# First token tile's queries alone in the opening, values turned in their own bank, GpSimd makes the context's low parts

## The reference

```python
q = (layernorm(x) @ Wq)            # 512 tokens, 32 heads of 16
k, v = context @ Wk, context @ Wv  # per batch 512 keys, 8 heads of 16
x = x + softmax(q k^T / 4) v @ Wo
x = x + self_attention(layernorm(x))      # 2nd layer: rope, causal, 32 heads on 8
w = block_dequantize_3bit(q3, norm)       # (bits / 7) * (2 n) - n
x = x + layernorm(x) @ w.T + bias
```

## Time and profile before

| | us |
|---|---|
| median of 3 runs | 336.38 (335.36 to 337.74) |
| profiled execution | 338.57 |
| span of its instructions | 336.7 |
| PE busy in it | 312.5 (93%) |
| DVE, ACT, POOL busy | 228.4, 186.6, 111.0 |

### The profile page before, as it was taken

How to read it: one execution, slowest core, us unless ns; L and a number is a source line. 1 busy time by engine, 2 the same in 40 slices (tenths; PEclk the granted TensorE clock), 3 DMA queues, 4 the chain that set the end, 5 groups by cost and what they waited for, 6 DMA issues and landing times.

```text
span 336.7 us, 7756 instructions
## 1 busy us (share of the span) xinstructions
PE 312.5 (93%) x2662; PEld 217.2 (64%) x2665; DVE 228.4 (68%) x391; ACT 186.6 (55%) x368; POOL 111.0 (33%) x200
## 2 busy tenths in 40 slices
PE   6699939969999999999999999999999998999996
...
GB/s 212 412 191 22 135 112 74 202 181 86 180 118 188 180 104 197 185 88 200 184 92 205 182 117 227 181 156 201 146 0 5 2 6 6 9 6 8 2 31 93
DMA packets 39466, 41.48 MB, mean 123 GB/s; under 512 B 19936, under 2 KB 34272, under 8 KB 37216
## 3 DMA queue, kind: packets, MB, share of 16 engines
...
## 4 chain that ended last, share of the span: by engine, by line
PE 70%; DVE 12%; DMA 7%; ACT 4%; issue 3%; POOL 2%; SPq 1%; DVEq 0%; ACTq 0%; POOLq 0%
PE b_d L1001 8%; PE b_c L1059 7%; DMA kstack<-kparts 5%; PE b_v L976 4%; PE b_s L1022 4%; PE b_c L1187 4%; PE b_v L977 4%; PE b_v L978 4%; PE b_k L976 3%; PE b_k L978 3%; PE b_k L977 3%; PE b_x L1022 3%; DVE negmax L783 3%; DMA wkv_raw<-in_L_xattn_Wv_dram 2%; DVE vaug L773 2%
## 5 line engine op out<-in xcount | busy, mean ns | idle before, releaser
L591 ACT ACTIVATE region<-b_c 128x512 f32<-128x512 f32 x128 | 74.6, 597 | 46.3 <-PE b_c L1059 26.2
L783 DVE TENSOR_REDUCE negmax<-b_s 128x1 f32<-128x512 f32 x72 | 49.7, 690 | 49.4 <-PE b_s L1022 48.4
L1059 PE MATMUL b_c<-qstack,kstack 108*128 108x128 bf16 x512 | 50.6, 222 | 0.0
L795 DVE TENSOR_TENSOR cT_l<-cx,cT_h 128x512 fp32r<-128x512 f32 x56 | 45.1, 805 | 6.9 <-ACT cT_h L611 6.8
L1059 PEld LDWEIGHTS b_c<-qstack,kstack 108*128 108x128 bf16 x512 | 32.5, 98 | 26.6 <-issue 13.9
L976 PE MATMUL b_k<-cT_h,wkv_h 128*128 128x512 f32 x64 | 36.3, 568 | 7.8 <-DVE cT_l L827 4.2
L477 POOL TENSOR_TENSOR mwide<-negmax,zeros 128x4 bf16<-128x4 f32 x32 | 6.4, 199 | 101.4 <-DVE negmax L783 101.4
L783 DVE TENSOR_REDUCE negmax<-b_x 128x1 f32<-128x512 f32 x56 | 38.2, 681 | 0.9 <-PE b_x L1022 0.8
L976 PE MATMUL b_v<-cT_h,wkv_h 128*128 128x512 f32 x64 | 35.7, 558 | 1.6 <-DVE vaug L773 1.2
L611 ACT ACTIVATE cT_h<-cx 128x512 fp32r<-128x512 f32 x56 | 35.0, 628 | 0.0
L1022 PE MATMUL b_s<-kstack,qstack 96*128 96x512 bf16 x72 | 28.1, 391 | 6.4 <-DMA kstack<-kparts 3.3
(11 more groups left out here) (357 smaller groups left out, 584.7 us busy)
## 6 DMA issues: line engine op xcount, KB each, us to landing
...
```

The costliest lines, as they stand in the source:

```text
L591: nc.scalar.activation(pT[:, g], b_c[g % 2][:].rearrange("p (a n) -> p a n", a=KT), ACT.Exp, scale=SCALE).then_inc(exp_ready, 1)
L783: nc.vector.tensor_reduce(negmax[:, n % 2, g:g + 1], score_bank(n, g, trip)[:], AX, ALU.max, negate=True).then_inc(max_ready, 1)
L795: nc.vector.tensor_tensor(cT_l[:, c], cx[:, m % 2, c], cT_h[:, c].bitcast(F32), ALU.subtract).then_inc(ctx_low, 1)
L1059: last = nc.tensor.matmul(b_c[g % 2][:, P * a:P * a + P], kstack[0:ROWS, m % 4, g, P * a:P * a + P], qstack[0:ROWS, g, m % 4], start=True, ...
```

## The change

Four things are changed together.

- **Opening.** x is loaded in two DMAs, the first token tile alone. Only its queries are made ahead of slot 0 (`first_queries_of(0, ...)`, 16 matmuls of 128 columns); those of tiles 1 to 3 follow in slot 0, half a tile in each of its steps 0 to 5. A token tile holds four batches, so the first stacks are now six DMAs of 128 KB for batches 0 to 3 at once. Three chunks of batch 1's projections, the unpacking of the weights and the split of batch 1's keys move into slot 0. ACT converts batch 0's chunks 2 and 3 without waiting for the value weights.
- **Values.** `vT` is turned into bank `b_t` at g=5 (`turn_values`), DVE copies that bank at g=6. The next values in `b_v` wait for `vT` and no longer for DVE's copy. In the last slots `b_v` is used as before.
- **Context rests.** The operation on `cT_l` of batches 2 to 15 moves from DVE to POOL (`low_context`): chunk 0 at the start of POOL's slot, chunk 1 behind the keys' parts, chunks 2 and 3 behind the first half's maxima.
- **Weights.** DVE unpacks to 2q/7 - 1, and POOL multiplies once, in four parts, behind slot 1's work.

The diff, cut to what the text speaks of:

```diff
 
-            return g == 1 and (looped(trip) or 1 <= n < B - 1)
+            return g == 1 and (looped(trip) or n < B - 1)
 
         def wait_queries(eng, m, trip):
 
...
+                    eng.dma_start(qstack[HD * s:HD * s + HD].rearrange("p g b n -> p g (b n)"),
+                                  qparts[:, part, 0:BPT].rearrange("p b r t -> p (b r t)")).then_inc(first_queries, 16)
...
+        def value_bank(n, trip):
+
+            return b_t if looped(trip) or n < B - 2 else b_v
...
-                sp.dma_start(xs[:], xf).then_inc(x_loaded, 16)
+                sp.dma_start(xs[:, 0], xf[:, 0]).then_inc(x_loaded, 16)
                 sp.dma_start(xwq, xwq_d.rearrange("(c p) r n -> p c r n", p=P)).then_inc(xwq_loaded, 16)
+                sp.dma_start(xs[:, 1:TILES], xf[:, 1:TILES]).then_inc(xs_loaded, 16)
                 load_ctx(1, 0)
-                sp.wait_ge(ctx_low, C)
-                load_ctx(2, 0)
                 sp.dma_start(q3[:], q3_d.rearrange("(t p g) k -> p t (g k)", t=TILES, p=P)).then_inc(packed_loaded, 16)
-                sp.dma_start(wnorm[:, 0].rearrange("p (t g) -> p t g", t=TILES),
+                sp.dma_start(wnorm[:].rearrange("p (t g) -> p t g", t=TILES),
                              norm_d.rearrange("(t p g) a -> p t (g a)", t=TILES, p=P)).then_inc(packed_loaded, 16)
                 for i in range(2):
                     sp.dma_start(kstack[STACK:ROWS, i].bitcast(I32), sel_d).then_inc(first_sel, 16)
                 for part, done in enumerate((k_high, k_mid, k_low)):
                     sp.wait_ge(done, 1)
                     stack_keys(0, part)
-
+                sp.wait_ge(ctx_low, C)
+                load_ctx(2, 0)
+                for part, done in ((0, q_high), (2, q_low)):
+                    sp.wait_ge(done, 1)
+                    first_queries_part(sp, part)
                 sp.wait_ge(ctx_low, 2 * C)
                 load_ctx(3, 0)
-                for part, done in ((0, q_high), (2, q_low)):
-                    sp.wait_ge(done, R)
-                    first_queries_part(sp, part, 0, 1, first_queries)
-                for part in range(3):
-                    first_queries_part(sp, part, 1, 4, next_queries)
 
             def slot(n, trip):
                 if not looped(trip):
@@ -412,6 +417,8 @@
                     for part, done in enumerate((k_high, k_mid, k_low)):
                         sp.wait_ge(done, split)
                         stack_keys(m, part)
+                if not looped(trip) and n == 1:
+                    sp.wait_ge(q_low, TILES)
...
+            def low_context(m, c, trip):
+
+                if live(m, trip):
+                    wait(pool, ctx_high, C, m, c + 1, trip)
+                    if not looped(trip) and (m, c) == (2, 0):
+                        pool.wait_ge(ctx_low, 2 * C)
+                    nc.gpsimd.tensor_tensor(cT_l[:, c], cx[:, m % 2, c], cT_h[:, c].bitcast(F32), ALU.subtract).then_inc(ctx_low, 1)
+
             def slot(n, trip):
+                low_context(n + 2, 0, trip)
                 if live(n - 1, trip):
                     max_parts(n - 1, 1, trip)
                 if splits_keys(n, 1, trip):
                     key_parts(n + 1, trip)
+                low_context(n + 2, 1, trip)
                 if n == B - 1:
                     low_keys_values()
                 if live(n, trip):
                     max_parts(n, 0, trip)
+                low_context(n + 2, 2, trip)
+                low_context(n + 2, 3, trip)
+                if not looped(trip) and n == 1:
+                    pool.wait_ge(unpacked, 1)
+                    for t in range(TILES):
+                        scale_weights(t)
                 if n == B - 2:
...
-                pool.wait_ge(w_scaled, 1)
-                pool.wait_ge(unpacked, 1)
-                nc.gpsimd.tensor_tensor(wide, wide, wnorm[:, 1].unsqueeze(2).to_broadcast([P, NGRP, GS]), ALU.mult).then_inc(w_step, 1)
-                key_parts(1, 0)
-                pool.wait_ge(w_step, 1)
-                nc.gpsimd.tensor_tensor(wide, wide, wnorm[:, 0].unsqueeze(2).to_broadcast([P, NGRP, GS]), ALU.subtract).then_inc(w_ready, 1)
 
             opening()
             slots(pool, slot, 2)
...
+                    if not looped(trip) and n == 0 and g in (2, 4, 6):
+                        query_high(g // 2)
+                    if not looped(trip) and n == 0 and g in (3, 5, 7):
+                        query_mid(g // 2)
...
             def opening():
                 act.wait_ge(wk_loaded, 16)
                 nc.scalar.activation(wkv_h[:, 0], wkv_raw[:, 0], ACT.Copy).then_inc(wk_high, 1)
-                context(0, 0)
-                context(0, 1)
+                for c in range(C):
+                    context(0, c)
                 act.wait_ge(wv_loaded, 16)
                 nc.scalar.activation(wkv_h[:, 1], wkv_raw[:, 1], ACT.Copy).then_inc(wv_high, 1)
-                context(0, 2)
-                context(0, 3)
+                act.wait_ge(eps_ready, 1)
+                deviation1(slice(0, 1))
+                key_high(0, 0)
                 act.wait_ge(ident_loaded, 16)
                 nc.scalar.activation(ident_h[:], ident[:], ACT.Copy).then_inc(identh_ready, 1)
...
+                rows_turned(0)
                 act.wait_ge(v_chunk, C)
                 nc.scalar.activation(vT[:], b_v[:], ACT.Copy).then_inc(vT_ready, 1)
-                for t in range(TILES):
-                    act.wait_ge(xh_transposed, t + 1)
-                    nc.scalar.activation(xhT[:, :, P * t:P * t + P], (b_x, b_s, *b_c)[t][:].rearrange("p (c n) -> p c n", c=C),
-                                         ACT.Copy).then_inc(xhT_ready, 1)
+                deviation1(slice(1, TILES))
                 context(1, 0)
                 context(1, 1)
                 query_high(0)
+                rows_turned(1)
+                query_mid(0)
+                act.wait_ge(q_mid, 1)
+                first_queries_part(act, 1)
+                rows_turned(2)
+                rows_turned(3)
                 context(1, 2)
-                query_mid(0)
-                query_high(1)
                 context(1, 3)
-                query_mid(1)
-                for r in (2, 3):
-                    query_high(r)
-                    query_mid(r)
-                act.wait_ge(q_mid, R)
-                first_queries_part(act, 1, 0, 1, first_queries)
-                key_high(1, 0)
...
+                    if not looped(trip) and n == 0 and g in (2, 4, 6):
+                        query_residue(g // 2)
+                    if not looped(trip) and n == 0 and g in (3, 5, 7):
+                        query_low(g // 2)
+                    if not looped(trip) and n == 0 and g < 6:
+                        unpack(g)
                     if splits_keys(n, g, trip):
 
                         key_residue(n + 1, trip)
                     if g == 4 and live(n - 2, trip):
                         normalise(n - 2, trip)
-                    if g == 4 and live(n + 1, trip):
-                        copy_values(n + 1, trip)
-                    if g % 2 == 0 and live(n + 2, trip):
-
-                        m, c = n + 2, g // 2
-                        wait(dve, ctx_high, C, m, c + 1, trip)
-                        nc.vector.tensor_tensor(cT_l[:, c], cx[:, m % 2, c], cT_h[:, c].bitcast(F32), ALU.subtract).then_inc(ctx_low, 1)
+                    if g == 6 and live(n + 1, trip):
+                        copy_values(n + 1, value_bank(n, trip), trip)
...
+                statistics(range(1, TILES))
+                dve.wait_ge(ln1_rstd, 2)
+                normalise1(range(1, TILES))
                 context(1, 0)
                 context(1, 1)
-                unpack(0)
-                unpack(1)
                 query_residue(0)
+                query_low(0)
+                copy_values(0, b_t, 0)
                 context(1, 2)
-                query_low(0)
...
+                    pe.wait_ge(w_ready, 4)
+                    pe.wait_ge(v_ready, B - 1)
...
-                    wait(pe, v_ready if which else k_res, 1, m, 0, trip)
+                    wait(pe, vT_ready if which else k_res, 1, m, 0, trip)
...
+            def turn_values(m, bank, trip):
+
+                wait(pe, vT_ready, 1, m, 1, trip)
+                wait(pe, v_ready, 1, m, 0, trip)
+                for a in range(KT):
+                    last = nc.tensor.transpose(bank[:, P * a:P * a + P], vT[:, P * a:P * a + P], ident[:])
+                last.then_inc(v_transposed, 1)
+
             def projections(n, g, trip):
 
-                if not looped(trip) and (n, g) in ((0, 0), (0, 1), (0, 3)):
-                    return []
...
+            def first_queries_of(t, rows):
+
+                pe.wait_ge(xhT_ready, t + 1)
+                count(pe, q_res, t - 1)
+                for r in rows:
+                    for c in range(C):
+                        last = nc.tensor.matmul(b_c[t % 2][:, P * r:P * r + P], xwq[:, c, r], xhT[:, c, P * t:P * t + P],
```

(40 more changed lines are left out.)

132 lines of the change are left out of this document (64 added, 68 removed).

## The result

The changed kernel takes 352.28 us (median of 4, 350.32 to 352.70), the kernel before on the same chip 337.06: **ratio 1.044, 95% interval 1.038 to 1.051, slower**. Forecast were 336.5 us, no change, with a range of 328 to 346. The profiled execution of the changed kernel took 351.98 us, its span is 350.1, 13.4 over the span of before.

A forecast was written before the change was run, and what follows sets the result against it. The middle was taken as bound by PE's own work in its order, the start by query matmuls, DVE and key transfers. Terms: -9.6 us ahead of slot 3, +9.6 in slots 3 to 13, giving 336.5 us; range 328 to 346.

The forecast's parts named there:

- Values in their own bank: Steps g=4 and g=5: PE no longer idles for vT's turning and DVE's copy; gain 0.59 us per slot.
- GpSimd's chunk ahead of the maxima: Slots 2 to 13, g=1: PE waits 1.46 us per slot for POOL's maxima behind chunk 0; slots of 13.75.
- some 0.2 after the next slot wants it: Steady slots: chunk 3 on POOL ends about 0.2 us late for the next slot, inside the slack.
- rival that POOL doesn't hold PE: Steady slots: maxima are in time after all, slots of 12.29, 319 us in all; chance 0.1.
- the one with the clock: Rival: PE's clock falls once in each steady slot, costing 1.7 us a slot, 357 us in all; chance 0.1.
- The chunk's price: One context-rest operation on POOL takes 1.16 us, with 1.27 as the other bound.
- The opening: Ahead of slot 3: an earlier slot 0 and moved work save 9.6 us, known to +-5.
- slot 0 begins at about 30.5: First score: six 128 KB stacks at 1.15 us each land from about 24 us on; ends 28.5 and 33.
- Slot 0 itself: Slot 0: 18.4 us of PE work at full clock plus 2.5 for a lower clock, ending at 51.4.
- No POOL delay there: Slot 1: chunk 0 of batch 3 is ready early, keys land in time, slot takes 10.8 us.
- The scaling ... used in slot 14: nothing: Behind slot 1: POOL's four weight-scaling operations cost nothing, since their result is used only in slot 14.
- From slot 14 to the end the change moves nothing: Last 109 us: nothing found on the path that the change moves, so this stretch stays.

The follow-up runs named there:

- experiment 4: The kernel before, with only the values' turning changed: own bank at g=5, copied at g=6; 335.29 us, ratio 0.991.
- Experiment 6: The kernel before, with only the context rests of batches 2 to 15 moved to GpSimd, chunk 0 ahead of the maxima; 352.02 us, ratio 1.045.
- Experiments 9 to 11: On experiment 8: first stacks of 32 KB (325.93 us); context 2's 1 MB load behind the stacks (328.30 us); both (321.34 us).
- experiment 8: The changed kernel with maxima ahead of chunk 0, scaling spread inside slot 1, rests of batches 4 to 15 on VectorE; 329.93 us, ratio 0.979.
- Experiment 12: On experiment 8: small first stacks, context 2 behind them, no ACT transfers in the opening, context 1's third chunk made earlier; 319.44 us, ratio 0.947.
- experiment 1: The changed kernel, with the second half's maxima ahead of chunk 0 on GpSimd; 337.67 us, ratio 1.000 to the kernel before.
- experiment 5: The changed kernel with only its opening kept: values in their old bank, all context rests on VectorE; 335.22 us, ratio 0.989.
- Experiment 2: The changed kernel, with the four weight-scaling operations spread inside slot 1 on GpSimd instead of at its end; 346.22 us, ratio 1.031.

## Why the prediction was wrong

**Values in their own bank: right.** Forecast 0.59 a slot. Steps g=4 and 5 together are 0.64 shorter, in experiment 4 too, where g=1 gives 0.2 to 0.3 of it back.

**GpSimd's chunk ahead of the maxima: right.** Forecast 1.46 us a slot and slots of 13.75. Experiment 6 has 1.42 a slot over eleven and 1.4 to 1.5 in most; the change has 13.65. The split was not as told: 0.3 us of it, at g=0, is a wait of 0.4 for the rest of chunk 3, which I had seen as "some 0.2 after the next slot wants it" and taken to be inside the slack. Slots 3 to 13 came to 150.2 for a forecast of 151.3. The rival that POOL doesn't hold PE fell with it, and so did the one with the clock: 0.95 us of idle PE in every slot, and the clock row of the middle says 1.00. On this the Trainium skill (TensorE: Matmul & The Clock Gate, A second HAM failure mode) speaks of small waits that make the clock swing; in the middle of this kernel the trace does not agree. In slots 1 and 2 the clock fell, behind waits of 1.38 and 3.88.

**The chunk's price: low.** I took 1.16 us by the bf16 row with 1.27 as the other end; it is 1.29 in the mean of 56. Against VectorE's 0.69 that is 1.86 times, and the Trainium skill's 1.96 (GPSIMD Engine Reference, Performance versus the Vector engine) was nearer than my 1.7; my other end, 1.27 us, was nearer still. It moved little.

**The opening: this failed.** The step "slot 0 begins at about 30.5" came from six stacks of 1.15 us each, as if nothing were ahead of them (24 and six times 1.15 also make 30.9). The 1 MB of context 2 was, and slot 0 began at 33.64: +3.1. I had noted that the engines were full in a stretch before it and then not charged what was issued ahead. Experiments 9 to 11 show it: with the 1 MB behind the stacks and nothing else changed the first score is at 31.86, against experiment 8's 34.27. That is 2.4 us. The rest is PE's own work, which I had ended at 28.5 and which ended at 31.13: it waited 3.56 us for chunk 2 of batch 1, which ACT makes behind its two transfers and the turned rows, and worked at half clock behind that. Experiment 12, with ACT's order changed as well, begins slot 0 at 26.50. Slot 0 itself was right, 21.4 for 20.9; a query matmul took 0.11 us (1.78 for 16), the end that I had chosen.

**"No POOL delay there", slot 1: failed.** Forecast 10.8, measured 13.9. Chunk 0 of batch 3 was not ready early: ACT makes its half at 56.81, behind a piece of the last queries and the maxima's rows, and these wait for VectorE. So POOL takes chunk 0 at 57.52 and the maxima behind it come 1.38 us late; ACT's rows for the first products come 0.79 late, and then the clock is low for 3.4 us (PE is busy 11.72 us, against 10.48 in experiment 1, where it stays up: 1.2 lost). Experiment 1 took only 0.9 back: with the maxima ahead PE waits 1.7 us for POOL's chunks instead, and still 0.79 for ACT. Nor was the slot short without rests on POOL (14.17 in experiment 5, waiting for keys); 11.31 in experiment 6 is the only one near the forecast.

**"The scaling ... used in slot 14: nothing": failed, and is the largest single error.** Slot 2 took 17.9 for 13.75. I looked at who waits for the result and not at who stands behind it on POOL. The rule was in the working for chunk 0 and not applied to the scaling. Experiment 2 gives all of it back (4.3), and experiment 5 shows that without the rests on the same queue it would have been free.

**"From slot 14 to the end the change moves nothing": failed**, +3.7. The load of the queries' weights waits for batch 15's last rest, one of the operations that the change moves, so it is issued 1.35 us later. That used up the slack, and a transfer 2.7 us longer than before did the rest. How much of the 3.7 belongs to the change can't be said: by experiment 6 it may be nothing. So this step failed, and its cause is open in part.

The sum: +3.1, +0.5, +3.1, +4.1, -1.1, +3.7 = 13.4 us, which is the whole difference (each is a difference of two rows of the table above). The forecast had one term for GpSimd's queue in a steady slot, and four places outside it where the same mechanism, or a transfer's place in a queue, had to be looked for.
